# Query stacks transposed by DMA, later weight loads, zero matmuls in early gaps, and a minimum in PSUM in place of the second layer's mask matmul, in a two-layer attention and feed-forward kernel

## The reference, cut to what matters

```python
scores = jnp.where(mask[:, None, :, :] == 0, NEG, scores)           # layer 0, per sequence
probs = jax.nn.softmax(scores, axis=-1)
energy = jnp.where(mask == 0, jnp.float32(-1e+20), energy)          # layer 1, one mask
attention = jax.nn.softmax(energy / jnp.float32(EMBED ** 0.5), axis=3)
out = jnp.einsum('nhqk,nkhd->nqhd', attention, vh).reshape(N, qlen, EMBED) @ Wo.T + bo
```

## Time and profile before

| what | value |
|---|---|
| median of 3 runs | 214.71 us (214.35 to 215.3) |
| the profiled execution's own time | 216.64 us |
| its span, first to last instruction | 214.8 us |
| TensorE matmul busy | 196.6 us, 92% |
| TensorE weight loads busy | 160.8 us, 75% |
| VectorE busy | 162.4 us, 76% |
| ScalarE busy | 135.3 us, 63% |
| GpSimd busy | 82.7 us, 38% |
| mean granted TensorE clock | 0.987 |

### The profile page before, as it was taken

The page is one execution under the profiler, slowest core; times in us unless marked ns, Lnnn a source line. Parts: engine busy times, 40 slices in busy tenths (PEclk is TensorE's granted clock), DMA queues, the critical chain, the costliest instruction groups (busy, mean ns, idle before and its releaser), DMA issues.

```text
span 214.8 us, 6119 instructions
## 1 busy us (share of the span) xinstructions
PE 196.6 (92%) x2114; PEld 160.8 (75%) x2114; DVE 162.4 (76%) x608; ACT 135.3 (63%) x378; POOL 82.7 (38%) x197
## 2 busy tenths in 40 slices
PE   2487697999999999999999999999999999999992
PEld 0255474757766777777888988898979889999992
DVE  6458989999999999999987859966576736265225
ACT  3343466468868677766968579547955576566430
POOL 4494320432337544143520425438210604232532
PEclk9999889999999999999999999999999999999998
DMA  5849678504440724430080000400220000000000
GB/s 156 243 111 303 164 98 349 145 9 101 108 92 0 160 50 92 98 87 17 2 92 9 5 0 17 98 3 12 54 47 6 0 15 0 17 0 15 2 10 24
DMA packets 39747, 15.09 MB, mean 70 GB/s; under 512 B 34211, under 2 KB 38819, under 8 KB 39462
## 3 DMA queue, kind: packets, MB, share of 16 engines
q1 hardware_dynamic: 39142, 14.00, 27.7%
q10 hardware_dynamic: 576, 0.72, 1.0%
HBM read 5.80 MB, written 0.52 MB: 29 GB/s over the span
## 4 chain that ended last, share of the span: by engine, by line
PE 81%; DVE 7%; DMA 5%; issue 2%; SPq 2%; POOL 1%; ACT 1%; DVEq 0%; ACTq 0%
PE ps_B L826 14%; PE ps_A L839 12%; PE ps_O L756 7%; PE ps_B L690 7%; PE ps_A L675 6%; PE ps_B L692 6%; PE ps_Q L708 6%; PE ps_A L677 6%; DMA m0T_i<-in_mask0T 5%; PE ps_O L764 3%; PE ps_X L722 2%; PE ps_A L791 2%; PE ps_O L774 2%; PE ps_A L835 2%; PE ps_P L736 2%
## 5 line engine op out<-in xcount | busy, mean ns | idle before, releaser
L907 ACT ACTIVATE probs<-ps_B 128x512 f32<-128x512 f32 x64 | 36.5, 598 | 15.6 <-PE ps_B L692 14.8
L956 ACT ACTIVATE hid<-ps_B,b_sb 128x128 f32<-128x128 f32 x128 | 35.6, 378 | 15.3 <-PE ps_B L826 15.2
L1063 DVE TENSOR_REDUCE mx<-ps_A 128x4 f32<-128x512 f32 x64 | 42.0, 677 | 3.7 <-PE ps_A L677 3.7
L826 PE MATMUL ps_B<-mxT,w_sb 128*128 128x128 f32 x256 | 33.3, 278 | 0.0
L839 PEld LDWEIGHTS ps_A<-w_sb,hid 128*128 128x128 f32 x256 | 31.1, 192 | 0.6
L839 PE MATMUL ps_A<-w_sb,hid 128*128 128x128 f32 x256 | 31.2, 275 | 0.0
L826 PEld LDWEIGHTS ps_B<-mxT,w_sb 128*128 128x128 f32 x256 | 30.6, 192 | 0.5 <-issue 0.4
L654 POOL TENSOR_TENSOR yc<-yc 128x512 f32<-128x512 f32 (+2 forms) x21 | 17.3, 823 | 34.1 <-DVE yc L1228 33.0
L675 PE MATMUL ps_A<-m_b,id_b 128*128 128x512 bf16 x64 | 24.7, 385 | 2.4 <-DVE mx L1063 1.2
L692 PEld LDWEIGHTS ps_B<-qmT,kblk 118*128 118x128 bf16 x256 | 20.4, 100 | 8.6 <-issue 0.8
L692 PE MATMUL ps_B<-qmT,kblk 118*128 118x128 bf16 x256 | 25.5, 223 | 0.0
(11 more groups left out here) (135 smaller groups left out, 391.5 us busy)
## 6 DMA issues: line engine op xcount, KB each, us to landing
w_sb<-in_m1T SPq DMA_DIRECT2D x1, 1024.0 KB, 6.2
w_sb<-in_m2T SPq DMA_DIRECT2D x1, 1024.0 KB, 8.1
out_y<-out_sb SPq DMA_DIRECT2D x8, 64.0 KB, 1.5
x_sb<-in_x SPq DMA_DIRECT2D x1, 448.0 KB, 6.7
ctx_sb<-in_ctxT ACTq DMA_DIRECT2D x1, 448.0 KB, 5.5
m_i<-in_mask SPq DMA_DIRECT2D x1, 384.0 KB, 4.2
m0T_i<-in_mask0T SPq DMA_DIRECT2D x1, 384.0 KB, 5.0
kblk<-kst SPq DMA_TRANSPOSE x16, 3.7
```

What stands on the lines that cost most here:

```text
L826: mm = pe.matmul(psum("z", b, i)[:, c * P:(c + 1) * P], w1_sb[:, 4 * i + c, :], mxT[:, b % 2, :], start=True, stop=True)
L907: ends(act.activation(probs[:, n % 2, 4 * i:4 * i + 4, :], psum("exp", n, i)[:, :].rearrange("p (h k) -> p h k", h=4), ACT.Exp, scale=ATTN ...
L956: ins = act.activation(hid[:, b % 2, 4 * i + c, :], psum("z", b, i)[:, c * P:(c + 1) * P], ACT.Relu, bias=b1_sb[:, 4 * i + c:4 * i + c + 1])
L1063: ends(dve.tensor_reduce(mx[:, n % 2, 4 * i:4 * i + 4], psum("max", n, i)[:, :].rearrange("p (h k) -> p h k", h=4), AX.X, ALU.max), "dve.max")
```

## The change

1. **Query stacks by DMA in layer 1.** `pe.qs`/`act.qs` and `pe.qb`/`act.qb` stay in layer 0 alone. In layer 1 SyncE issues a DMA transpose from qst into qT (`sp.qs`) and one into qmT (`sp.qb`). The stacks and their transposed copies get more buffers (4, 3 and 3 for 3, 2 and 2).
2. **The mask of layer 1's shifted scores.** The mask matmul at L690 stays in layer 0 alone. In layer 1 a new step `dve.pm` takes, in PSUM and in place, the minimum of each 128x512 group of shifted scores and a limit per key and query, and ScalarE's exponential waits for it. The limit is made once (`pe.mc`, `dve.lm`).
3. **Rounding on ScalarE.** `dve.xr` and `dve.hr` become `act.xr` and `act.hr`.
4. **Loads.** x and the context come in halves (sequences 1 to 3, then 4 to 7), the masks in four parts (0; 1; 2 and 3; 4 to 7), the weights of layer 0 behind the key transpose of unit 3, those of layer 1 behind that of unit 4, the expert weights in four parts behind those of units 5 to 8.
5. **Zero matmuls.** 25 matmuls of zeros, each 128x512 bf16, into ps_B's second bank ahead of twelve early TensorE steps (FILLERS).
6. **Order.** UNIT_ORDER has (1, 0) and (1, 1) later by one place, TIME, START, BIAS and ARRIVES have new values, and START has six values for each unit, one for each stage. Some buffers share memory, and one zeroing of kst moves from VectorE to GpSimd.

```diff
-UNIT_ORDER = ((0, 0), (0, 1), (0, 2), (0, 3), (0, 4), (0, 5), (1, 0), (1, 1), (0, 6), (0, 7), (1, 2),
+UNIT_ORDER = ((0, 0), (0, 1), (0, 2), (0, 3), (0, 4), (0, 5), (0, 6), (1, 0), (0, 7), (1, 1), (1, 2),
               (1, 3), (1, 4), (1, 5), (1, 6), (1, 7))
+QUERY_STACK = ((("pe.qs", 1, "pool.ql"), ("act.qs", 1, "pe.qs")),
+               (("sp.qs", 1, "pool.ql"),))
+SHIFTED_STACK = ((("pe.qb", 1, "dve.m3"), ("act.qb", 1, "pe.qb")),
+                 (("sp.qb", 1, "dve.m3"),))
...
-    ("pe.exp", 4, "act.qb"),
-    ("act.exp", 4, "pe.exp"),
+    ("pe.exp", 4, SHIFTED_STACK[l][-1][0]),
+    *((("dve.pm", 4, "pe.exp"),) if l else ()),
+    ("act.exp", 4, ("pe.exp", "dve.pm")[l]),
...
+FILLERS = {("kv", 0, 0): 6, ("xT", 0, 0): 3, ("q", 0, 0): 1, ("kv", 1, 0): 2, ("xT", 1, 0): 4,
+           ("xT", 2, 0): 3, ("xT", 3, 0): 1, ("q", 2, 0): 1, ("max", 0, 0): 1, ("max", 2, 2): 1,
+           ("max", 2, 3): 1, ("max", 3, 0): 1}
...
-            sp.dma_start(x_sb[:, 1:NB, :], x[1:NB].rearrange("b t d -> t b d")).then_inc(s_x, 16)
+            sp.dma_start(x_sb[:, 1:4, :], x[1:4].rearrange("b t d -> t b d")).then_inc(s_x, 16)
...
                 if n == 0:
+                    masks(1, 1, 2)
                     sp.dma_start(wo_sb[0][:, :], w0o).then_inc(s_wo, 16)
+                    sp.dma_start(x_sb[:, 4:NB, :], x[4:NB].rearrange("b t d -> t b d")).then_inc(s_x4, 16)
                 if n == 1:
-                    masks(1, 2, NB)
+                    masks(2, 2, 4)
+                    sp.dma_start(ctx_sb[:, 4:NB, :], ctxT[:, 4:NB, :]).then_inc(s_ctx4, 16)
+                if n == 2:
+                    masks(3, 4, NB)
+                if n == 3:
                     for k, src in enumerate((wg, wu, wd)):
...
+                if n in (5, 6, 7, 8):
+                    part = slice(4 * (n - 5), 4 * (n - 5) + 4)
+                    sp.dma_start(w1_sb[:, part, :], m1T[:, part, :]).then_inc(s_moe, 16)
+                    sp.dma_start(w2_sb[:, part, :], m2T[:, part, :]).then_inc(s_moe, 16)
-            masks(0, 0, 2)
+            masks(0, 0, 1)
...
+                if name == "qs":
+                    after(sp, "pool.ql", n)
+                    if n >= TSLOTS:
+                        after(sp, "pe.max", n - TSLOTS)
+                    if b >= 2:
+                        wait_landed(sp, b - 2, "qs")
+                    sp.dma_start_transpose(qT[:, n % TSLOTS, :, :], qst[:, n % QSLOTS, :, :].rearrange("p g c -> p (g c)")
+                                           ).then_inc(landed["qs"][b % 2], 16)
...
-                m = (m0T_b[:, b, :] if l == 0 else m1T_b[:, :]).unsqueeze(1).broadcast_to([P, 4, P])
-                pe.matmul(o[:, :].rearrange("p (h k) -> p h k", h=4), id_b[:, :], m, start=True, stop=False)
+                if l == 0:
+                    pe.matmul(o[:, :].rearrange("p (h k) -> p h k", h=4), id_b[:, :],
+                              m0T_b[:, b, :].unsqueeze(1).broadcast_to([P, 4, P]), start=True, stop=False)
...
+            def fill(count):
+                for _ in range(count):
+                    pe.matmul(banks["B"][1][:, :].rearrange("p (h k) -> p h k", h=4), fill_b[:, :],
+                              fill_b[:, :].unsqueeze(1).broadcast_to([P, 4, P]), start=True, stop=True)
...
+                if name == "hr":
+                    after(act, "dve.h3", b)
+                    if b >= 1:
+                        after(act, "dve.hq", b - 1)
+                    ends(act.activation(hr[:, :], z2[:, b % 2, :], ACT.Copy, bias=ROUND, scale=fs[:, b, 11:12]), "act.hr")
...
+                if name == "pm":
+                    after(dve, "pe.exp", n, i)
+                    if b == 0 and i == 0:
+                        after(dve, "dve.lm", 0)
+                    o = psum("exp", n, i)[:, :].rearrange("p (h k) -> p h k", h=4)
+                    ends(dve.tensor_tensor(o, o, limit[:, :].unsqueeze(1).broadcast_to([P, 4, P]), ALU.min), "dve.pm")
```

More of the change, by code:

```diff
@@ L118 @@
     ("dve.fn", 1, "pool.fp"),
-)
+) for l in range(2)]
 STEPS = (
-    (("dve.mk", 1),) + ATTENTION + (
+    (("dve.mk", 1),) + ATTENTION[0] + (
         ("dve.q0", 1, "dve.fn"),
@@ L177 @@
     ("pool.m1", 1),
+    ("pe.mc", 1, "pool.m1"),
+    ("dve.lm", 1, "pe.mc"),
     ("dve.bp", 5),
@@ L187 @@
[L187 to L192, removed]
@@ L204 @@
[L204 to L208, removed]
+    "dve.st": (0.22, 0.3), "dve.ag": (0.1, 0.19), "pool.pw": (0.92, 0.92), "dve.nm": (0.2, 0.31),
@@ L262, in steps_of @@
+LAYER_TIME = ({}, {"pe.exp": (0.24, 0.34)})
+GROUP = {name: k for k, names in enumerate(STAGES) for name in names.split()}
 def steps_of(n):
@@ L287, in ready @@
             if n >= ring:
-                needs.append((reader, n - ring, parts[0][reader] - 1))
+                if reader == "stack.qb":
+                    reader = SHIFTED_STACK[UNIT_ORDER[n - ring][0]][0][0]
+                needs.append((reader, n - ring, (parts[0].get(reader) or parts[1][reader]) - 1))
         for ring, reader in LAYER_SLOTS[l].get(name, ()):
@@ L781, in _ @@
                     ends(pe.matmul(psum("wm", 0)[:, 0:3], ones[:, :], wf_sum[:, :], start=True, stop=True), "pe.wm")
+                if name == "mc":
+                    after(pe, "pool.m1", 0)
+                    wait_free(pe, "mc", 0)
+                    ends(pe.matmul(psum("mc", 0)[:, 0:P], ones[:, :], m1_k[:, :], start=True, stop=True), "pe.mc")
                 if name == "fxT":
@@ L885, in _ @@
                     after(act, "pe.q", n)
-                    if n >= 3:
-                        after(act, "pe.qb", n - 3)
+                    if n >= QSLOTS and units[n - QSLOTS][0] in BY_DMA:
+                        wait_landed(act, units[n - QSLOTS][1], "qb")
+                    elif n >= QSLOTS:
+                        after(act, "pe.qb", units[n - QSLOTS][1])
                     elif n:
@@ L1051, in _ @@
                                            ALU.subtract), "dve.rk")
+                    if n == 0:
+                        dve.memset(banks["O"][0][:, :], 0.0).then_inc(bank_zero, 1)
                 if name == "rq":
@@ L1114, in _ @@
                     if b >= 2 and l == 0:
-                        after(dve, "dve.xr", b - 2)
+                        after(dve, "act.xr", b - 2)
                     if b >= 2 and l == 1:
@@ L1156, in _ @@
                     if b >= 2:
-                        after(dve, "dve.hr", b - 2)
+                        after(dve, "act.hr", b - 2)
                     ends(dve.tensor_tensor(z2[:, b % 2, :], z1[:, :], psum("up", b)[:, :], ALU.mult), "dve.up")
@@ L1237, in _ @@
                                            apply_absolute_value=True), "dve.ws")
+                if name == "lm":
+                    after(dve, "pe.mc", 0)
+                    last_part(dve.tensor_scalar(limit[:, :], m1_k[:, :], -1.0, 0.0, ALU.mult, ALU.add))
+                    ends(dve.scalar_tensor_tensor(limit[:, :], psum("mc", 0)[:, 0:P], P * MASKED, limit[:, :],
+                                                  ALU.add, ALU.max), "dve.lm")
+                if name == "pm":
[4 more added lines that the diff above has]
+                    ends(dve.tensor_tensor(o, o, limit[:, :].unsqueeze(1).broadcast_to([P, 4, P]), ALU.min), "dve.pm")
                 if name == "wm": weight_means()
```

317 lines of the change are left out of this document (184 added, 133 removed), and 7 rows, old and new, of the table START.

## The result

The changed kernel takes 216.01 us (median of 20 runs, 214.59 to 217.2) for 214.69 us before (20 runs): a ratio of 1.0048 with a 95% interval of 1.0026 to 1.007, so 1.0 us slower where 13.1 us less were forecast. Its profiled execution has a span of 214.1 us, 0.7 us less than that of before; the runs are the measure.

What follows compares the result with a forecast made beforehand. TensorE was taken to bound the kernel from 24 to 190 us; -13.9 (TensorE) - 2.0 (start) - 1.7 (clock) + 4.5 (VectorE) = -13.1 us, from a median of 214.71 to 201.6 us, range 195.5 to 211 us.

Steps and rivals of the forecast that it cites:

- in that stage what TensorE no longer does is worth its distance in the issue order: From 24 to 190 us: mask matmuls 7.0 us and query stacks 7.2 us off TensorE, together 13.9 us less with the limit's matmul.
- The DMA's latency: Layer 1's query stacks: ready 2.7 us later by DMA than on TensorE and ScalarE, 16 times, 43 us if nothing covers it.
- The VectorE term: From 24 to 190 us: minima bring VectorE's work level with TensorE's, so 4.5 us are added over TensorE's bound.
- The clock: After 24 us: zero matmuls in early gaps keep TensorE's granted clock up, a gain of 1.7 us at no cost.
- The start: First 24 us: smaller early loads of masks, x and context shrink two mask waits, a gain of 2.0 us.
- ScalarE's roundings: Layer 0: eight of about 0.60 us and eight of 0.28 us move to ScalarE; nothing counted for the added crossing.
- VectorE sets the pace, with gaps: Rival, 24 to 190 us: minima wait for TensorE in VectorE's fixed order; at 93% busy, 209 us; chance 0.22.
- Late stacks: Rival, layer 1: DMA query stacks arrive late and hold TensorE; 223 us with half of each open; chance 0.09.
- What TensorE saves comes back as waits on late steps elsewhere: No-change rival: the planner's new order uses guessed times; time stays within half a per cent of 214.71 us; chance 0.04.
- The signs: In the changed profile, wrong if: qT or qmT waits over 2 us, minima 0.8 us or more, shifted-score waits over 5 us, misplaced fillers.

Runs made afterwards that it cites:

- the other order of the same work: The changed kernel with all its instructions and loads, its steps reordered by a new search with its planner's rules: 216.83 us, 1.0093 of the kernel before.
- one moved chain: The changed kernel with the three steps that make the limit (pool.m1, pe.mc, dve.lm) moved later, all else kept: 216.0 us, 1.0046 of the kernel before.

## Why the prediction was wrong

**What failed first is the step "in that stage what TensorE no longer does is worth its distance in the issue order".** I put 13.9 us on it. Alone on the old order, 7.0 us of mask matmuls were worth 3.2 us and 6.3 us of transposes 2.1 us. The table I had read shows why in part: from 60 to 90 us VectorE was full as well, which I noted and left out of the price, and over the whole of 24 to 110 us it was at 96%, and at 97% in an execution whose clock didn't fall. Up to 110 us the missing mask matmuls brought 0.7 of 2.6 us. A busy share of 98% says that an engine has no gaps, not that nothing else would make gaps once it is faster. Behind 110 us, where VectorE had room, they brought 2.5 of 4.4 us; why not all, the runs don't tell.

**The DMA's latency was put at nothing in the sum and stood in a rival alone.** On the old order it is some 6.6 us. On the new one TensorE has no listed wait for a DMA of qT or qmT. Whether the latency is paid for in where the steps stand was not tested.

**The VectorE term, 4.5 us**, was mis-sized on both sides: the minima cost 17.5 us on the old order, 11.3 us there with the DMA stacks, and 2.4 us on the new one. What one pass takes was right: 0.69 us long, 0.60 us to the next start in the changed kernel, for 0.61 us:

```profile
119.81 0.69 DVE L1356 TENSOR_TENSOR ps_B<-ps_B,limit 128x512 f32<-128x512 f32 x1
120.41 0.68 DVE L1179 TENSOR_REDUCE mx<-ps_A 128x4 f32<-128x512 f32 x1
```

What I had priced too low is the hand-over from TensorE to VectorE to ScalarE with a bank held meanwhile, on a list that isn't arranged for it: the 25.0 and 6.0 us of waits above.

**The clock, 1.7 us**, was read off one execution that isn't typical. The profiled execution had a fall of the clock, which I priced at 1.7 us, and I took these off a median of runs that mostly lack it. The 1.9 us between that execution and the median, which I had noted, are about what the fall costs. Measured on the old order: no change, anything from 0.7 us less to 0.8 us more. On the new order the fillers are worth 3.7 us, more than I counted. There the clock does fall: 18 of the changed kernel's 20 executions have a mean granted clock of 0.991 or less, 12 of them 0.989 to 0.991 with a median of 215.9 us and 6 of them 0.982 to 0.984 with one of 216.8 us; the other two have 0.996 and 214.6 and 214.8 us. Within one kernel more time goes with a lower clock. That the clock makes up the 1.0 us isn't shown: the other order of the same work has a clock of 1.00 in its profile, and takes 1.0 us more still. **The start, 2.0 us**, was not tested on the old order; on the new one the old loads cost 4.0 us, which has the forecast sign.

**ScalarE's roundings** I costed at 0.60 and 0.28 us a piece and nothing on the path. They last 0.73 and 0.41 us; alone they make the old order 1.6 us slower, and undone they make the new one 5.3 us slower.

**The rivals.** The nearest is "VectorE sets the pace, with gaps": it named 93% busy, and 93% is what VectorE shows from 24 to 170 us. But its time of 209 us fell 7 us short, its sign was VectorE waiting over 5 us for shifted scores, where the profile has 0.7 us, and VectorE's added work is a small part of the cause: without the minima the new order still takes 213.5 us. Late stacks had the right side and price on the old order (4.5 us more), and not the signs that I had asked for in the changed kernel. "What TensorE saves comes back as waits on late steps elsewhere", the case to which I gave 0.04, describes the changed kernel best: 9.7 us more of idle TensorE from 24 to 150 us in small waits for neighbours, and a clock of 0.94 for 30 us, which is 1.8 us more. Its bound, half a per cent, holds the measured 0.48%.

**The signs** that I had named for being wrong didn't show either: TensorE had no such wait on qT or qmT, the minima stayed below 0.8 us, VectorE waited 0.7 us for shifted scores. Those for being right were near: VectorE busy for 173.1 us (I had said 175 to 178), TensorE for 192.9 us (190 or less), a clock of 1.00 from 24 to 36 us. All of them look at the price of single steps. What told the outcome, TensorE idle in many small waits, was none of them.

**The account that the runs bear.** Put on the old order the minima and the DMA stacks together cost 14.3 us, and the roundings 1.6 us; the changed kernel is 1.0 us slower. So the new order and the new loads win back an estimated 15 us of what the parts cost on an order that is not made for them. This is a sum over parts, and the parts didn't add where it was tested. And on the new order each of the five parts that were undone cost 3.4 to 8.8 us. Two engines at 93% and 91% side by side, with hand-overs among five, are where both orders of this work ended. **What stays open** is how the loss of the changed kernel divides among its parts, and whether an order exists that turns TensorE's saved time into less time. Neither the new search nor one moved chain found it, and no kernel that does all the work was faster than the one before.

## What to carry to other kernels

In a kernel whose engines run hand-made lists, the price of an instruction is that of the place where it stands: measure what a microsecond off the fullest engine brings, by leaving one such instruction out, before you exchange it for work on the second-fullest. Before you put a price on something seen in one profile, such as a fall of the clock, look whether the other executions have it. Read how full the second engine is in the same stage as the first, since that is what is left of the gain. And test a part both ways, put into the old kernel and taken out of the new one; where both cost time, as the roundings, the DMA stacks and the minima did here, it is the arrangement that is being measured, not the part.

## What was unexpected of the hardware

ScalarE's copy with a scale per partition and an added constant, from SBUF to SBUF, lasts 728 ns for 128x512 and 406 ns for 128x128, where its passes from PSUM without the constant last 0.59 to 0.60 and 0.28 us. A VectorE pass that reads and writes the same PSUM bank lasts 689 ns, no longer than one from PSUM to SBUF. A DMA transpose of a query stack, half the size of a key stack, lands in 2.7 to 2.8 us at the median, for 3.7 us, and takes 1.23 us to issue. The granted clock of one and the same kernel differs between executions: the one before had 0.995 to 1.00 in 62 of 70 and 0.988 to 0.992 in 8, which were 1.6 us longer at the median.
